# Experts on plain float32 matmuls, zero rows earlier, the last bias on VectorE

## The chip, the cores and the metric

The kernel runs on one core of a Trainium2 chip. The metric is the device time of one execution in microseconds. The kernel before took 3154.27 us in the median of three runs (3150.88 to 3159.85). One further execution was recorded with the hardware profiler; all rows come from it.

## The reference, cut to what matters

The input x has 16 sequences of 512 rows of 256 numbers (8192 rows). With a layer norm before each half, the reference computes

```
xn = layernorm(x)
x  = x + fast_weights(xn) + ffn(xn)
xn = layernorm(x)
x  = x + attention(xn, 16 heads) + ternary_ffn(xn)

def ffn(u):                                  # 16 routed experts, 2 chosen per row
    s = softmax(u @ centroids.T + expert_biases)
    g = the two largest s of a row, at their experts, 0 elsewhere
    routed = sum_e g[e] * (u @ Wr[e].T + br[e])
    return u + routed + mean over 2 shared experts of (u @ Ws.T + bs)

def ternary_ffn(z):
    w = +1 / 0 / -1 by a threshold of 0.7 * mean(|weight|)
    return z @ (w * alpha).T + bias
```

All of it is float32. The attention normalises its input to unit root mean square first (rms_norm).

## The kernel before, in words

The program has four blocks, one after the other, each of which ends when all engines and all its transfers are done.

*route* (the sorting stage, L115 to L710) goes over 32 units of two row tiles (256 rows). It normalises rows, scores experts, computes the fast-weight part and the shared experts, and sends each normalised row by indirect DMA to two places in `rows_dram`, where each expert has a region of its own. The end of an expert's rows has to be filled with zero rows up to a full tile of 128. SyncE runs the loads and stores in the order of the code: for each step `v` of a software pipeline the store of `part`, loads, and at step `NU` the two transfers of the job table; behind all steps it waits for the scatters and then stores 16 blocks of zero rows, one per expert, at places that it reads from `ends_u` into a register (L264 to L266). The expert weights are loaded to `raw` during this stage.

*experts* (L713 to L864) goes over 144 jobs in 72 pairs. A job is a tile of 128 rows of one expert. First ScalarE rounds the weights to the reduced type float32r (`wr_hi`, L792) and VectorE subtracts to get the rest (`wr_lo`, L814), 8 pieces each; then both do the same for the row of biases (L795, L816). Per pair, TensorE transposes two tiles (L840), ScalarE makes `xt_hi` and VectorE `xt_lo` of them (L800, L820), and per tile TensorE reads the expert's column into a register (`value_load`, L855) and issues seven float32r matmuls of 256 columns: the bias through a selecting matrix (L857), then for both halves of the 256 inputs hi x hi, hi x lo, lo x hi (L861 to L863). ScalarE copies even pairs out of PSUM (L806), VectorE odd ones (L826). SyncE loads tiles three pairs ahead into a ring of eight (L758, a register load before each) and stores each pair (L770); its order is: two loads, wait for the copied pair, store. PSUM holds three pairs of results, so TensorE's pair n waits for the copy of pair n - 3.

*settle* (L867 to L1081) goes over 32 units of two tiles. VectorE adds the parts and the two gathered results of each row, computes mean and variance (L1016 to L1034), then calls `finish` for the unit before: it makes `xrt_lo` (L1000), waits for TensorE's eight matmuls with the ternary weights (L1079, L1080), and writes `base` (L1007); then it computes six small factors of its own unit (L1038 to L1047), for which GpSimd supplies two powers (L973, L974). GpSimd also adds the last bias (L976) and issues four indirect gathers (L961). ScalarE applies the factors (L986) and copies the transposed rows (L992). SyncE stores them and loads three units ahead.

*phase_b* is the attention, unchanged.

Of the kernel before, what the change touches and what calls it, by code (L numbers as in the profile page):

```python
# [21 lines left out]
F32 = mybir.dt.float32  # L22
# [5 lines left out]
P = 128  # L28
D = 256
# [79 lines left out]
def route(nc, io, rows, part, region, jobs, kept, raw, raw_in):  # L109
# [5 lines left out]
    with ExitStack() as ctx:  # L115
# [105 lines left out]
        def _(sp):  # L221
# [23 lines left out]
            for v in steps:  # L245
# [10 lines left out]
                if v == NU:  # L256
                    sp.wait_ge(tb_dve, 13)
                    for k in range(2):
                        sp.dma_start(kept.table[0:1, k * 2 * P:(k + 1) * 2 * P].rearrange("a (p h) -> a p h", p=P),
                                     jobs_u[:, k]).then_inc(tb_in, 16)  # L260

            for r in range(XN):
                sp.wait_ge(sent[r], 16 * TOP * TB * len(range(r, GN, XN)))
            for e in range(NE):  # L264
                at = sp.value_load(ends_u[0:1, e:e + 1], min_val=0, max_val=NE * region - P)
                sp.dma_start(rows[bass.ds(at, P), :], zeros[:]).then_inc(ends_in, 16)  # L266
# [446 lines left out]
def experts(nc, io, rows, results, region, jobs, kept, raw, raw_in):  # L713
    with ExitStack() as ctx:
# [6 lines left out]
        def bank(name, n=1):  # L721
# [15 lines left out]
        place_pool, br_in, zero_pool, split_act, split_dve, t_pe, t_act, t_dve, y_pe, y_act, y_dve = map(sem, (  # L737
            "place_pool", "br_in", "zero_pool", "split_act", "split_dve", "t_pe", "t_act", "t_dve", "y_pe", "y_act", "y_dve"))
        PAIRS = jobs // U
        CUT = 4  # L740
        WIDE = NE * D // CUT

# [11 lines left out]
        def _(sp):  # L754
# [5 lines left out]
            sp.dma_start(raw_br[:], io["br"].rearrange("(a e) n -> a (e n)", a=1)).then_inc(br_in, 16)  # L760
            for j in range(3 * U):
                load(j)
            for n in range(PAIRS):
                for t in range(U):
                    load((n + 3) * U + t)
                if n % 2 == 0:
                    need(sp, y_act, 1, n // 2, 1)
                else:
                    need(sp, y_dve, 1, n // 2, 1)
# [5 lines left out]
        def _(g):  # L775
            g.memset(brow[:].bitcast(F32), 0.0).then_inc(zero_pool, 1)
# [9 lines left out]
        @block.scalar  # L786
        def _(a):
            a.wait_ge(raw_in, 16 * 16)
            for c in range(CUT):
                for k in range(KD):  # L790
                    cols = slice(c * WIDE, (c + 1) * WIDE)
                    a.activation(wr[0][:, k, cols], raw[:, k, cols], ACT.Copy).then_inc(split_act, 1)  # L792
            a.wait_ge(zero_pool, 1)
            a.wait_ge(br_in, 16)
            a.activation(brow[0:1, :], raw_br[:], ACT.Copy).then_inc(split_act, 1)  # L795
            for n in range(PAIRS + 1):
                if n < PAIRS:
# [69 lines left out]
def settle(nc, io, results, part, xT_hi, xT_lo, base_dram, early, kept):  # L867
    NU = part.shape[0]
    with ExitStack() as ctx:
# [37 lines left out]
        def flat(ap):  # L907
            return ap.rearrange("p a b c -> p (a b c)")
# [820 lines left out]
```

## Time and profile before

| | us |
|---|---|
| median of three timed runs | 3154.27 |
| the profiled execution | 3168.83 |
| its span | 3167.0 |
| sorting stage, from 0 to | 401.3 |
| experts' stage, to | 637.5 |
| settling stage, to about | 932 |
| attention, to | 3167.0 |

The profiled execution took 14.6 us longer than the median of the timed runs. TensorE is busy for 89% of the span, and its granted clock was 0.939 of full speed in the mean; of the two levels, 1.2 and 2.4 GHz, a clock of 0.5 in a stretch is the lower and 1.0 the upper. A stage's limit has to be read in the stage itself, since the shares of the whole span are those of the attention, which is 70% of it.

### The profile page before, as it was taken

How to read it: one execution, taken by the hardware profiler on the slowest of the kernel's cores; microseconds unless marked ns; L12 is line 12 of the kernel's file. 1: busy time of each engine (PE TensorE's matmuls, PEld its weight loads, DVE VectorE, ACT ScalarE, POOL GpSimd, SP SyncE). 2: the span in 40 equal slices, each digit the busy share in tenths (PEclk: the TensorE clock that was granted, in tenths of full speed). 3: DMA queues.
4: the chain of work that ended last, by engine and by line, in shares of the span. 5: the costliest groups of instructions: out<-in, count | busy, mean ns of one | idle time of the engine just before them, and what ended most of it. 6: DMA issues, size and time to landing. Idle time of an engine off the chain costs nothing.

```text
span 3167.0 us, 48881 instructions
## 1 busy us (share of the span) xinstructions
PE 2803.9 (89%) x14290; PEld 2132.5 (67%) x14290; DVE 2115.3 (67%) x3500; ACT 1864.8 (59%) x2685; POOL 2058.2 (65%) x1314
## 2 busy tenths in 40 slices
PE   5888668834448999999999999999999999999997
PEld 4777557723336677777777777777777777777775
DVE  6888443356766666766767667677676667667664
ACT  4555232211126777777767767777776777777674
POOL 4666330077744777777777777777777777777775
PEclk8999879955559999999999999999999999999999
DMA  3432245577751222223222222222222232232222
GB/s 120 134 122 85 87 131 181 172 219 214 211 176 44 61 50 72 60 57 77 45 72 61 60 73 50 68 54 71 54 64 73 44 77 55 62 77 47 70 56 46
DMA packets 266847, 281.05 MB, mean 89 GB/s; under 512 B 96755, under 2 KB 205555, under 8 KB 266740
## 3 DMA queue, kind: packets, MB, share of 16 engines
q1 hardware_dynamic: 254452, 246.17, 29.4%
q0 software_dynamic: 12288, 33.57, 3.4%
q8 instruction: 54, 0.88, 0.1%
q14 instruction: 53, 0.43, 0.0%
HBM read 129.67 MB, written 82.31 MB: 67 GB/s over the span
## 4 chain that ended last, share of the span: by engine, by line
PE 66%; ACT 1%; DVE 1%; DMA 1%; POOL 1%; issue 1%; SPq 0%; POOLq 0%; ACTq 0%; DVEq 0%
PE psV_b L1601 7%; PE psV_b L1596 7%; PE psV_b L1597 7%; PE psS_b L1584 7%; PE psS_b L1583 7%; PE psN_b L1569 7%; PE psY_b L1524 4%; PE psX_b L1524 4%; PE psY_b L1525 4%; PE psY_b L1526 4%; PE psX_b L1525 4%; PE psX_b L1526 4%; POOL pp_lo_b L1314 1%; DMA xT_lo<-xT_lo_dram 1%; PE psN_b L1653 0%
## 5 line engine op out<-in xcount | busy, mean ns | idle before, releaser
L1314 POOL TENSOR_TENSOR pp_lo_b<-pf_b,pp_hi_b 128x1024 fp32r<-128x1024 f32 x512 | 1229.8, 2402 | 609.0 <-ACT pp_hi_b L1356 522.9
L1460 DVE TENSOR_REDUCE negmax_b<-psN_b 128x2 fp32r<-128x1024 f32 x512 | 627.2, 1225 | 379.2 <-PE psN_b L1569 371.6
L1351 ACT ACTIVATE pf_b<-psS_b 128x1024 f32<-128x1024 f32 x512 | 526.1, 1028 | 239.0 <-PE psS_b L1584 235.9
L1583 PE MATMUL psS_b<-qA_b,kA_b 128*128 128x512 f32 x1024 | 405.8, 396 | 6.6 <-DVE qB_b L1475 4.7
L1584 PE MATMUL psS_b<-qB_b,kB_b 68*128 68x512 f32 x1024 | 406.5, 397 | 0.0
L1597 PE MATMUL psV_b<-pp_hi_b,vals_lo_b 128*64 128x512 f32 x1024 | 403.8, 394 | 0.0
L1596 PE MATMUL psV_b<-pp_hi_b,vals_hi_b 128*65 128x512 f32 x1024 | 402.0, 393 | 1.5
L1569 PE MATMUL psN_b<-kA_b,qA_b 128*128 128x512 f32 x1024 | 322.7, 396 | 4.7 <-DVE negmax_b L1460 4.6
L1601 PE MATMUL psV_b<-pp_lo_b,vals_hi_b 128*65 128x512 f32 x1024 | 320.2, 394 | 5.0 <-POOL pp_lo_b L1314 5.0
L1375 ACT ACTIVATE kA_b<-psX_b 64x512 fp32r<-64x512 f32 x256 | 152.1, 594 | 290.0 <-PE psX_b L1526 285.1
L1356 ACT ACTIVATE pp_hi_b<-pf_b 128x1024 fp32r<-128x1024 f32 x256 | 271.5, 1060 | 8.1
L1449 DVE SCALAR_TENSOR_TENSOR kB_b<-psX_b,kA_b 64x512 fp32r<-64x512 f32 x256 | 176.2, 688 | 140.5 <-ACT kA_b L1375 136.5
L1583 PEld LDWEIGHTS psS_b<-qA_b,kA_b 128*128 128x128 f32 x1024 | 193.6, 189 | 65.6 <-DVE qB_b L1475 7.0
L1470 DVE CAST pp_hi_b<-pf_b 128x1024 fp32r<-128x1024 f32 x256 | 232.9, 910 | 5.3 <-ACT pf_b L1351 5.3
L1569 PEld LDWEIGHTS psN_b<-kA_b,qA_b 128*128 128x128 f32 x1024 | 192.2, 190 | 55.2 <-DVE negmax_b L1460 7.8
L1524 PE MATMUL psX_b<-xT_hi,wqkv_hi_b 128*128 128x512 f32 x512 | 210.7, 412 | 15.1 <-DVE wqkv_lo_b L1435 9.6
L1328 POOL TENSOR_TENSOR otf_b<-outs,inverse_b 128x512 f32<-128x512 f32 x128 | 210.3, 1643 | 18.5 <-DMA inverse_b<-inverse_dram 15.1
L1584 PEld LDWEIGHTS psS_b<-qB_b,kB_b 68*128 68x128 f32 x1024 | 193.6, 189 | 40.5
L1601 PEld LDWEIGHTS psV_b<-pp_lo_b,vals_hi_b 128*65 128x65 f32 x1024 | 137.9, 135 | 105.3 <-POOL pp_lo_b L1314 8.9
L1525 PE MATMUL psX_b<-xT_lo,wqkv_hi_b 128*128 128x512 f32 x512 | 203.8, 398 | 0.0
L1526 PE MATMUL psX_b<-xT_hi,wqkv_lo_b 128*128 128x512 f32 x512 | 203.4, 397 | 0.0
L1475 DVE TENSOR_TENSOR qB_b<-psN_b,own_tile_b 4x512 fp32r<-4x512 f32 x256 | 173.3, 677 | 43.0 <-PE psN_b L1653 40.7
(243 smaller groups left out, 6123.1 us busy)
## 6 DMA issues: line engine op xcount, KB each, us to landing
kA_b<-kA_b SPq DMA_DIRECT2D x128, 256.0 KB, 3.2
qB_b<-qA_b SPq DMA_DIRECT2D x128, 256.0 KB, 2.9
inverse_b<-inverse_dram SPq DMA_DIRECT2D x256, 128.0 KB, 3.1
xs_e<-rows_dram SPq DMA_DIRECT2D x144, 128.0 KB, 2.1
results_dram<-ys_e SPq DMA_DIRECT2D x72, 256.0 KB, 2.3
x_a<-x_dram SPq DMA_DIRECT2D x16, 512.0 KB, 4.7
part_dram<-acc_a SPq DMA_DIRECT2D x32, 256.0 KB
acc_s<-part_dram SPq DMA_DIRECT2D x32, 256.0 KB
```

What stands on the lines that cost most here:

```text
L1314: pool.tensor_tensor(pp[1][:, c], pf[:, c], pp[0][:, c].bitcast(F32), ALU.subtract).then_inc(pl_pool, 1)
L1351: a.activation(pf[:, c], psS[:], ACT.Exp).then_inc(exp_act, 1)
L1460: v.tensor_reduce(negmax[:, n.slot(2), 2 * c:2 * c + 2], psN[:], AX.X, ALU.max, negate=True).then_inc(mx_dve, 1)
L1524: pe.matmul(out, lh, rh, start=start, stop=False)
L1525: pe.matmul(out, lh, rl, start=False, stop=False)
L1526: return pe.matmul(out, ll, rh, start=False, stop=stop)
L1569: mm = pe.matmul(psN[:, t], qA[:, s, i * P:(i + 1) * P], kA[:, s], start=True, stop=True)
L1583: pe.matmul(psS[:, t], kA[:, s, keys], qA[:, s], start=True, stop=False)
L1584: mm = pe.matmul(psS[:, t], kB[:, s, keys], qB[:, s], start=False, stop=True)
L1596: pe.matmul(psV[0:DH + 1, g.slot(2)], values(0, h, i), pp[0][:, c, t], start=(i == 0), stop=False)
L1597: pe.matmul(psV[0:DH, g.slot(2)], values(1, h, i), pp[0][:, c, t], start=False, stop=False)
L1601: mm = pe.matmul(psV[0:DH + 1, g.slot(2)], values(0, h, i), pp[1][:, c, t], start=False, stop=(i == TB - 1))
```

## The change

It has four parts. The 16 stores of zero rows go out in the last two steps of the sorting stage, eight each. In the experts' stage the weights are used as they were loaded: plain float32 matmuls, two per tile, without the conversion of weights and biases and without `xt_lo`; the biases of all experts are loaded to every partition (`bias_bc`), and VectorE adds them when it copies a result out of PSUM, one tile at a time, at a column that it reads into a register. In the settling stage GpSimd's two powers become one instruction of twice the columns, the add of the last bias goes from GpSimd to VectorE, and `finish` is cut in two: `xrt_lo` stays where it was, and `base` is written behind the factors.

```diff
+                if NU <= v < NU + 2:
+                    for e in range((v - NU) * NE // 2, (v - NU + 1) * NE // 2):
+                        at = sp.value_load(ends_u[0:1, e:e + 1], min_val=0, max_val=NE * region - P)
+                        sp.dma_start(rows[bass.ds(at, P), :], zeros[:]).then_inc(ends_in, 16)
 
             for r in range(XN):
                 sp.wait_ge(sent[r], 16 * TOP * TB * len(range(r, GN, XN)))
-            for e in range(NE):
-                at = sp.value_load(ends_u[0:1, e:e + 1], min_val=0, max_val=NE * region - P)
-                sp.dma_start(rows[bass.ds(at, P), :], zeros[:]).then_inc(ends_in, 16)
...
-        wr = [sb(f"wr_{p}", [P, KD, NE * D], F32R) for p in ("hi", "lo")]
-        brow = sb("brow", [P, NE * D], F32R)
-        raw_br = sb("raw_br", [1, NE * D])
+        bias_bc = sb("bias_bc", [P, NE * D])
         xs = sb("xs", [P, XS, D])
-        xt = [sb(f"xt_{p}", [P, 2, U, KD, P], F32R) for p in ("hi", "lo")]
+        xt = sb("xt", [P, 2, U, KD, P])
...
-            sp.dma_start(raw_br[:], io["br"].rearrange("(a e) n -> a (e n)", a=1)).then_inc(br_in, 16)
             for j in range(3 * U):
                 load(j)
+            sp.dma_start(bias_bc[:], io["br"].rearrange("e n -> (e n)").partition_broadcast(P)).then_inc(br_in, 16)
             for n in range(PAIRS):
                 for t in range(U):
                     load((n + 3) * U + t)
-                if n % 2 == 0:
-                    need(sp, y_act, 1, n // 2, 1)
-                else:
-                    need(sp, y_dve, 1, n // 2, 1)
+                need(sp, y_dve, U, n, U)
...
-            a.wait_ge(raw_in, 16 * 16)
-            for c in range(CUT):
-                for k in range(KD):
-                    cols = slice(c * WIDE, (c + 1) * WIDE)
-                    a.activation(wr[0][:, k, cols], raw[:, k, cols], ACT.Copy).then_inc(split_act, 1)
-            a.wait_ge(zero_pool, 1)
-            a.wait_ge(br_in, 16)
-            a.activation(brow[0:1, :], raw_br[:], ACT.Copy).then_inc(split_act, 1)
-            for n in range(PAIRS + 1):
-                if n < PAIRS:
-                    need(a, t_pe, 1, n, 1)
-                    need(a, y_pe, 1, n - 2, 1)
-                    a.activation(flat(xt[0][:, n % 2]), psT[:, n % 2], ACT.Copy).then_inc(t_act, 1)
-                m = n - 1
-                if m >= 0 and m % 2 == 0:
-                    need(a, y_pe, 1, m, 1)
-                    if m >= 4:
-                        a.wait_ge(y_out[m % 4], 16 * (m // 4))
-                    a.activation(ys[:, m % 4].rearrange("p a b -> p (a b)"), psY[:, m % 3], ACT.Copy).then_inc(y_act, 1)
+            for n in range(PAIRS):
+                need(a, t_pe, 1, n, 1)
+                need(a, y_pe, 1, n - 2, 1)
+                a.activation(flat(xt[:, n % 2]), psT[:, n % 2], ACT.Copy).then_inc(t_act, 1)
...
-            for c in range(CUT):
-                for k in range(KD):
-                    cols = slice(c * WIDE, (c + 1) * WIDE)
-                    v.wait_ge(split_act, c * KD + k + 1)
-                    v.tensor_tensor(wr[1][:, k, cols], raw[:, k, cols], wr[0][:, k, cols].bitcast(F32), ALU.subtract).then_inc(split_dve, 1)
-            v.wait_ge(split_act, CUT * KD + 1)
-            v.tensor_tensor(brow[32:33, :], raw_br[:], brow[0:1, :].bitcast(F32), ALU.subtract).then_inc(split_dve, 1)
             for n in range(PAIRS + 1):
-                if n < PAIRS:
-                    need(v, t_act, 1, n, 1)
-                    v.tensor_tensor(flat(xt[1][:, n % 2]), psT[:, n % 2], flat(xt[0][:, n % 2]).bitcast(F32), ALU.subtract).then_inc(t_dve, 1)
                 m = n - 1
-                if m >= 0 and m % 2 == 1:
+                if m >= 0:
+                    at = [v.value_load(kept.table[0:1, m * U + t:m * U + t + 1], min_val=0, max_val=(NE - 1) * D) for t in range(U)]
+                    if m == 0:
+                        v.wait_ge(br_in, 16)
                     need(v, y_pe, 1, m, 1)
                     if m >= 4:
                         v.wait_ge(y_out[m % 4], 16 * (m // 4))
-                    v.tensor_copy(ys[:, m % 4].rearrange("p a b -> p (a b)"), psY[:, m % 3]).then_inc(y_dve, 1)
+                    for t in range(U):
+                        v.tensor_tensor(ys[:, m % 4, t], psY[:, m % 3, t * D:(t + 1) * D], bias_bc[:, bass.ds(at[t], D)],
+                                        ALU.add).then_inc(y_dve, 1)
...
+                    need(pe, t_act, 1, n - 2, 1)
...
-            pe.wait_ge(split_dve, CUT * KD + 1)
+            pe.wait_ge(raw_in, 16 * 16)
             for n in range(PAIRS):
                 turn(n + 1)
-                need(pe, t_dve, 1, n, 1)
-                if n >= 3:
-                    if (n - 3) % 2 == 0:
-                        need(pe, y_act, 1, (n - 3) // 2, 1)
-                    else:
-                        need(pe, y_dve, 1, (n - 3) // 2, 1)
+                need(pe, t_act, 1, n, 1)
+                need(pe, y_dve, U, n - 3, U)
                 for t in range(U):
                     j = n * U + t
                     at = pe.value_load(kept.table[0:1, j:j + 1], min_val=0, max_val=(NE - 1) * D)
                     out = psY[:, n % 3, t * D:(t + 1) * D]
-                    pe.matmul(out, kept.pick[:], brow[:, bass.ds(at, D)], start=True, stop=False)
                     for k in range(KD):
-                        left = [part[:, n % 2, t, k] for part in xt]
-                        right = [part[:, k, bass.ds(at, D)] for part in wr]
-                        pe.matmul(out, left[0], right[0], start=False, stop=False)
-                        pe.matmul(out, left[0], right[1], start=False, stop=False)
-                        mm = pe.matmul(out, left[1], right[0], start=False, stop=(k == KD - 1))
+                        mm = pe.matmul(out, xt[:, n % 2, t, k], raw[:, k, bass.ds(at, D)], start=(k == 0), stop=(k == KD - 1))
...
-            g.wait_ge(const_in, 16)
             for u in range(NU):
                 need(g, s_dve, SD, u, 9)
                 need(g, s_dve, SD, u - 2, SD)
-                g.tensor_tensor(vs[:, u % 2, 0], mv[:, u % 2, :, 1], eps[:], ALU.add).then_inc(s_pool, 1)
+                g.tensor_tensor(vs[:, u % 2], mv[:, u % 2, :, 1].unsqueeze(1).to_broadcast([P, 2, U]), eps[:], ALU.add).then_inc(s_pool, 1)
                 need(g, s_pool, SP, u, 1)
-                g.tensor_tensor(root[:, u % 2, 0], vs[:, u % 2, 0], power[:, 0], ALU.pow).then_inc(s_pool, 1)
-                g.tensor_tensor(root[:, u % 2, 1], mv[:, u % 2, :, 1], power[:, 1], ALU.pow).then_inc(s_pool, 1)
-                need(g, o_dve, U, u - 3, U)
-                g.tensor_tensor(x1b[:, u % 3], x1[:, u % 3], fbias_bc[:].unsqueeze(1).to_broadcast([P, U, D]),
-                                ALU.add).then_inc(s_pool, 1)
+                g.tensor_tensor(flat2(root[:, u % 2]), flat2(vs[:, u % 2]), flat2(power[:]), ALU.pow).then_inc(s_pool, 1)
                 gather(u + 3)
...
+            def rows_low(u):
+                if u < 0:
+                    return
+                need(v, t_act, 1, u, 1)
+                if u >= 2:
+                    v.wait_ge(stored[u % 2], 80 * (u // 2))
+                v.tensor_tensor(flat(xrt[1][:, u % 2]), psT[:, u % 2], flat(xrt[0][:, u % 2]).bitcast(F32),
+                                ALU.subtract).then_inc(t_dve, 1)
+
             def finish(u):
                 if u < 0:
                     return
-                need(v, t_act, 1, u, 1)
-                v.tensor_tensor(flat(xrt[1][:, u % 2]), psT[:, u % 2], flat(xrt[0][:, u % 2]).bitcast(F32),
-                                ALU.subtract).then_inc(t_dve, 1)
-                need(v, s_pool, SP, u, 4)
-                if u >= 2:
-                    v.wait_ge(stored[u % 2], 80 * (u // 2))
                 need(v, f_pe, 1, u, 1)
                 for t in range(U):
                     v.scalar_tensor_tensor(out=base[:, u % 2, t], in0=psF[:, u % 2, t * D:(t + 1) * D], scalar=fac[:, u % 3, 5, t:t + 1],
                                            in1=x1b[:, u % 3, t], op0=ALU.mult, op1=ALU.add).then_inc(o_dve, 1)
 
+            v.wait_ge(const_in, 16)
...
+                need(v, s_pool, SP, u - 2, 2)
                 for t in range(U):
                     v.bn_aggr(mv[:, u % 2, t], stats[:, u % 2, t]).then_inc(s_dve, 1)
-                finish(u - 1)
+                rows_low(u - 1)
+                v.tensor_tensor(x1b[:, u % 3], x1[:, u % 3], fbias_bc[:].unsqueeze(1).to_broadcast([P, U, D]),
+                                ALU.add).then_inc(s_dve, 1)
                 f = fac[:, u % 3]
-                need(v, s_pool, SP, u, 3)
+                need(v, s_pool, SP, u, 2)
                 v.tensor_tensor(f[:, 0], root[:, u % 2, 0], root[:, u % 2, 1], ALU.mult).then_inc(s_dve, 1)
...
                 v.scalar_tensor_tensor(out=f[:, 4], in0=mv[:, u % 2, :, 0], scalar=-1.0, in1=f[:, 3],
                                        op0=ALU.mult, op1=ALU.mult).then_inc(s_dve, 1)
+                finish(u - 1)
+            rows_low(NU - 1)
             finish(NU - 1)
```

## Rows read from the trace of the kernel before

**Rows 1.** Windows by stage: start:end, length; busy (instructions) per engine; clock, DMA share, GB/s.

```profile
401.30:425.00 23.70, 8.53 (x39) 7.77 (x40) 16.11 (x12) 13.46 (x13) 22.21 (x18) 0.51 0.20 58
425.00:630.00 205.00, 182.07 (x1237) 152.31 (x1236) 71.38 (x104) 58.54 (x103) 8.94 (x16) 0.99 0.57 175
...
650.00:925.00 275.00, 122.83 (x496) 98.69 (x496) 190.14 (x573) 53.73 (x96) 206.00 (x247) 0.54 0.68 205
```

**Rows 2.** SyncE's two DMA lines: count, ns min/median/max, first to last start.

```profile
L758 SPq DMA_DIRECT2D xs_e<-rows_dram x144: 332/333/1283, 402.9 to 625.9; - x144
...
L770 SPq DMA_DIRECT2D results_dram<-ys_e x72: 360/383/1208, 422.7 to 634.9; - x72
```

**Rows 3.** Timeline of TensorE, experts (start us, us, instruction): full clock, then half clock.

```profile
501.89 0.60 PE L840 MATMUL psT_e<-ident_f,xs_e 128*128 128x128 f32 x4
...
504.43 0.28 PE L862 MATMUL psY_e<-wr_lo_e,xt_hi_e 128*128 x1
504.55 0.28 PE L863 MATMUL psY_e<-wr_hi_e,xt_lo_e 128*128 x1
504.67 0.60 PE L840 MATMUL psT_e<-ident_f,xs_e 128*128 128x128 f32 x4
...
446.71 0.41 PE L863 MATMUL psY_e<-wr_hi_e,xt_lo_e 128*128 x1
446.92 0.41 PE L857 MATMUL psY_e<-brow_e,pick 128*128 x1
```

**Rows 4.** Timeline of SyncE's queue, end of sorting and first experts.

```profile
376.96 1.22 SPq L259 DMA_DIRECT2D table<-jobs_u_a  x2
...
382.79 16.71 SPq L266 DMA_DIRECT2D rows_dram<-zeros_a  x16
...
402.93 8.04 SPq L758 DMA_DIRECT2D xs_e<-rows_dram  x8
...
426.07 0.38 SPq L770 DMA_DIRECT2D results_dram<-ys_e  x1
427.20 1.43 SPq L758 DMA_DIRECT2D xs_e<-rows_dram  x2
428.68 0.43 SPq L770 DMA_DIRECT2D results_dram<-ys_e  x1
```

**Rows 5.** VectorE's first add of a settling unit: count, ns, first to last start.

```profile
L1016 DVE TENSOR_TENSOR acc_s<-psA_s,x_s x32: 691/692/693, 649.6 to 914.1; 128x512 f32<-128x512 f32 x32
```

**Rows 6.** Timeline of one unit of the settling stage.

```profile
768.31 0.69 DVE L1016 TENSOR_TENSOR acc_s<-psA_s,x_s 128x512 f32<-128x512 f32 x1
...
771.88 0.66 DVE L1000 TENSOR_TENSOR xrt_lo_s<-psT_s,xrt_hi_s 128x512 fp32r<-128x512 f32 x1
...
772.32 0.73 POOL L973 TENSOR_TENSOR root_s<-vs_s,power_s 128x2 f32<-128x2 f32 x1
...
774.25 0.41 PE L1080 MATMUL psF_s<-wtern,xrt_lo_s 128*128 128x256 f32 x1
...
774.81 0.88 DVE L1007 SCALAR_TENSOR_TENSOR base_s<-psF_s,fac_s,x1b_s 128x256 f32<-128x256 f32 x2 [2.27 <-DMA xT_lo_dram<-xrt_lo_s]
...
775.60 0.15 DVE L1038 TENSOR_TENSOR fac_s<-root_s 128x2 f32<-128x2 f32 x1
...
776.91 0.69 DVE L1016 TENSOR_TENSOR acc_s<-psA_s,x_s 128x512 f32<-128x512 f32 x1
```

**Rows 7.** DMA throughput of the first 40 us, in 40 slices of 1 us.

```profile
GB/s 0 8 63 370 386 364 229 63 135 235 348 361 366 374 368 344 337 319 312 253 122 378 60 0 0 0 0 0 0 48 241 236 0 0 8 0 0 0 0 0
```

**Rows 8.** Groups of TensorE, sorting stage, 80 to 340: count, busy us, mean ns.

```profile
L706 PE MATMUL psB_a<-th_a,w_a 128*128 128x256 f32 x206 | 52.9, 379 | 0.0
...
L704 PE MATMUL psB_a<-pick,bshare_a 128*128 128x256 f32 x52 | 14.7, 283 | 0.0
```

**Rows 9.** Two lines of GpSimd: count, ns min/median/max, first to last start.

```profile
L334 POOL TENSOR_TENSOR rstd_a<-rstd_a,power_a x16: 1007/1008/1040, 7.3 to 302.3; 128x4 f32<-128x4 f32 x16
...
L782 POOL TENSOR_TENSOR moved_e<-moved_e,shift_e x15: 453/458/4663, 408.9 to 434.5; 128x128 f32<-128x128 f32 x15
```

More of the change, by code:

```diff
@@ L736, in experts @@
         y_out = [sem(f"y_out{i}") for i in range(4)]
-        place_pool, br_in, zero_pool, split_act, split_dve, t_pe, t_act, t_dve, y_pe, y_act, y_dve = map(sem, (
-            "place_pool", "br_in", "zero_pool", "split_act", "split_dve", "t_pe", "t_act", "t_dve", "y_pe", "y_act", "y_dve"))
+        place_pool, br_in, t_pe, t_act, y_pe, y_dve = map(sem, (
+            "place_pool", "br_in", "t_pe", "t_act", "y_pe", "y_dve"))
         PAIRS = jobs // U
-        CUT = 4
-        WIDE = NE * D // CUT
         def flat(ap):
@@ L775, in _ @@
         def _(g):
-            g.memset(brow[:].bitcast(F32), 0.0).then_inc(zero_pool, 1)
             g.tensor_copy(moved[:], kept.place_f[:]).then_inc(place_pool, 1)
@@ L834, in turn @@
                         need(pe, x_in[j % XS], 16, j // XS, 16)
-                    need(pe, t_dve, 1, n - 2, 1)
+                    need(pe, t_act, 1, n - 2, 1)
                     for t in range(U):
@@ L881, in settle @@
         power = sb("power", [P, 2, U])
-        eps = sb("eps", [P, U])
+        eps = sb("eps", [P, 2, U])
         acc = sb("acc", [P, 4, U, D])
@@ L903, in settle, with flat2 @@
             "const_in", "const_pool", "s_dve", "s_pool", "p_pe", "x_act", "t_pe", "t_act", "t_dve", "f_pe", "o_dve"))
-        SD = 5 + 2 + 2 + 6
-        SP = 4
+        SD = 5 + 2 + 2 + 1 + 6
+        SP = 2
         def flat(ap):
             return ap.rearrange("p a b c -> p (a b c)")
+        def flat2(ap):
+            return ap.rearrange("p a b -> p (a b)")
         block = ctx.enter_context(nc.Block())
@@ L950, in _ @@
         def _(g):
-            for tile, value in ((power[:, 0], -0.5), (power[:, 1], 0.5), (eps[:], 1e-5)):
+            for tile, value in ((power[:, 0], -0.5), (power[:, 1], 0.5), (eps[:, 0], 1e-5), (eps[:, 1], 0.0)):
                 g.memset(tile, value).then_inc(const_pool, 1)
-            g.wait_ge(const_pool, 3)
+            g.wait_ge(const_pool, 4)
             def gather(u):
@@ L1013, in _ @@
                 need(v, x_act, U, u - 3, U)
-                need(v, s_pool, SP, u - 3, 4)
                 need(v, p_pe, 1, u, 1)
@@ L1031, in _ @@
                 need(v, s_dve, SD, u, 7)
-                need(v, s_pool, SP, u - 2, 3)
+                need(v, s_pool, SP, u - 2, 2)
                 for t in range(U):
                     v.bn_aggr(mv[:, u % 2, t], stats[:, u % 2, t]).then_inc(s_dve, 1)
-                finish(u - 1)
+                rows_low(u - 1)
+                v.tensor_tensor(x1b[:, u % 3], x1[:, u % 3], fbias_bc[:].unsqueeze(1).to_broadcast([P, U, D]),
+                                ALU.add).then_inc(s_dve, 1)
                 f = fac[:, u % 3]
-                need(v, s_pool, SP, u, 3)
+                need(v, s_pool, SP, u, 2)
                 v.tensor_tensor(f[:, 0], root[:, u % 2, 0], root[:, u % 2, 1], ALU.mult).then_inc(s_dve, 1)
-                need(v, s_dve, SD, u, 10)
+                need(v, s_dve, SD, u, 11)
                 v.tensor_scalar(f[:, 1], f[:, 0], 1e-12 * float(D) ** -0.5, None, ALU.max).then_inc(s_dve, 1)
-                need(v, s_dve, SD, u, 11)
+                need(v, s_dve, SD, u, 12)
                 v.reciprocal(f[:, 2], f[:, 1]).then_inc(s_dve, 1)
                 v.tensor_scalar(f[:, 5], f[:, 1], kept.alpha_bc[:, 0:1], None, ALU.mult).then_inc(s_dve, 1)
-                need(v, s_dve, SD, u, 13)
+                need(v, s_dve, SD, u, 14)
                 v.tensor_tensor(f[:, 3], f[:, 2], root[:, u % 2, 0], ALU.mult).then_inc(s_dve, 1)
-                need(v, s_dve, SD, u, 14)
+                need(v, s_dve, SD, u, 15)
                 v.scalar_tensor_tensor(out=f[:, 4], in0=mv[:, u % 2, :, 0], scalar=-1.0, in1=f[:, 3],
                                        op0=ALU.mult, op1=ALU.mult).then_inc(s_dve, 1)
+                finish(u - 1)
+            rows_low(NU - 1)
             finish(NU - 1)
```

## The prediction, written before the result was known

> **What bounds the kernel now.** I read the page first: its forty slices show four stretches, a sorting stage to about 401 us, the experts' stage to about 637, a settling stage to about 932, and attention behind it, where TensorE is busy nine tenths and more. The edit touches the first three, so I asked for the windows of these stages. The reader is to see that TensorE is busy 182 of 205 us among the experts at full clock (0.99), and only 123 of 275 us in the settling stage, at half clock (0.54), where VectorE (190) and GpSimd (206) do more [rows 1]. Attention has 70% of the span and no instruction of it changes, so its time is carried over.
>
> Then I read each stage in order of time. *Experts:* 72 pairs of row tiles. The results of a pair are stored once per pair; first and last of these stores give (634.9 - 422.7) / 71 = 2.99 us per pair [rows 2]. A smooth pair is 504.67 - 501.89 = 2.78 us on TensorE [rows 3]: four transposes, 4 x (0.60 - 0.28) / 3 = 0.43 until the next may start, then per tile seven records at a pitch of 0.118 (0.83). The rest, 2.78 - 0.43 - 1.65 = 0.70, is idle around the two register loads that fetch the expert's column. SyncE runs nearly as long: store to store is 2.61 us where it never waits (426.07 to 428.68: 1.13 to the first load, 1.43 for two loads, 0.05) [rows 4]. *Settling:* 32 units in a loop that VectorE closes; 31 intervals take 914.1 - 649.6 = 264.5 us, 8.53 each, and the typical one 776.91 - 768.31 = 8.60 [rows 5, 6]. In it VectorE waits 2.27 us before L1007. The profile names a DMA of an older unit, but the last matmul into psF ends at 774.25 + 0.41 = 774.66, 0.15 before VectorE goes on, so it is the matmuls it waits for [rows 6].
>
> **Part 1, zero rows.** Before, SyncE issues the sixteen stores in (16.71 - 0.33) / 15 = 1.09 us each from 382.79, and the stage ends at 401.3, 1.8 us behind the last issue [rows 4, 1]. Now eight follow the table's transfers (done at 376.96 + 1.22 = 378.18), the last part store goes between (0.6), then the other eight: 378.2 + 16 x 1.09 + 0.6 + 1.8 = 398.1. Nothing on SyncE is behind them but the waits for scatters already sent, and the part store, 6 us later than before, is read only in the settling stage. **Saves 3.2 us**; bounds 0 (the stores held back by something else) and 4.6 (382.79 - 378.18).
>
> **Part 2, start of the experts.** Before, the first store goes 422.7 - 401.3 = 21.4 us into the stage: eight conversions on ScalarE and eight on VectorE, then the bias row, then 3.5 us of matmuls at half clock [rows 2, 1]. All that goes. What is late next is a new transfer: the biases on every partition, 128 x 16 KB = 2.1 MB, queued behind six loads. The loads start at 1.6 - 0.3 = 1.3 us, go out every (8.04 - 0.33) / 7 = 1.10 [rows 4], the last at 6.8; the bias is issued at about 7.3. The fastest slices at the kernel's start move 340 to 386 GB/s [rows 7]; at 366 the bias takes 5.7 us, with 2 us of landing (2.1 median for a load [rows 2]) it is there at 15. Pair 0's matmuls are done by about 12 even at half clock, so the bias ends last: two adds and the first store at 15.9. Loads 6 and 7 land behind the bias, at about 15, when TensorE wants them. **Saves 5.5 us**; bounds 0 (the bias at the 175 GB/s of this stage [rows 1] takes 12 us: store at 22) and 9 (only pair 0 decides).
>
> **Part 3, a pair in the steady stage.** Removed per tile: the bias matmul and six f32r records of 0.118. Added: two plain float32 matmuls. The sorting stage has this shape (L706, 128x128 by 128x256): 206 records stand there beside 52 of L704, where the code issues two plain ones for each, so a plain matmul is two records [rows 8]. Four records take 1.03 us and one 0.379, so the pitch is (1.03 - 0.379) / 3 = 0.217, and one plain matmul 0.434, against 3 x 0.118 = 0.354 for the three it replaces [rows 8, 3]. Per pair: 8 x 0.217 = 1.74 against 14 x 0.118 = 1.65. So the arithmetic gets 0.09 dearer, not cheaper; the gain must come from the idle 0.70. In the half-clock stretch at 446 us, records have a pitch of 0.21, and the second tile's L857 starts 0.21 behind the L863 before it, with no idle at all: the register load is done while slow records are still queued [rows 3]. Plain records are as slow (0.217) at full clock. I take 0.1 of the 0.70 as left: 0.43 + 1.74 + 0.1 = 2.27 us; bounds 2.2 and, nothing hidden, 2.87.
>
> VectorE gets all evictions: two adds of 128x256 from PSUM, which I put at 0.75 together (a 128x512 add from PSUM takes 0.69 at L1016 [rows 5]; bounds 0.69 and 0.88, the two of L1007 [rows 6]), and two register loads that lie before its wait for TensorE; with L820 gone it has room in 2.6 us. ScalarE keeps one copy. Then SyncE is late next: 2.61 us without a wait, more with its own slow issues (a load's issue is 0.333 median but 1.283 at most, a store's 0.383 and 1.208 [rows 2]); I add 0.14 for these. So 2.75 a pair: 71 x (2.99 - 2.75) = **17 us saved**. Bounds: 27 (2.61), and -6 (TensorE 2.87 and the 0.21 by which mean and smooth pair differ today: 3.08).
>
> **Part 4, settling.** VectorE's unit before: from the add at 768.31 to L1000's end at 772.54 are 4.23 us, then 2.27 of wait, 0.8 to the first small factor operation at 775.60, and 1.31 for the six of them [rows 6]. After: L1000, then the add of the bias (SBUF only, 128x512; 0.69 as L1016 [rows 5], bounds 0.6 and 0.88, the two of L1007 for as many columns [rows 6]), then the six factors, then the wait for psF, then L1007. GpSimd: its two powers (0.73 and 0.69) become one of four columns, which takes 1.008 in the sorting stage (L334 [rows 9]); it starts as today 4.01 into the unit (772.32) and ends at 5.0. Factors: 5.1 + 1.31 = 6.4. The matmuls start as today and end at 774.66 - 768.31 = 6.35, so L1007 may start at 6.5 as today. It takes 0.88, then the next unit: 7.4; with some friction 7.45. Its four transposes run on TensorE behind the matmuls, at the half-clock pitch of 0.21 [rows 3] some 0.9 us, to 7.25. GpSimd, busy 206 / 275 x 8.53 = 6.4 us of a unit [rows 1], loses the bias add and part of a power from that. The DMA engines go from 0.68 busy [rows 1] to 0.68 x 8.53 / 7.45 = 0.78. 31 intervals: 264.5 - 31 x 7.45 = 33.5, and the last unit gains some 1.5, as its factors no longer stand behind L1007. **Saves 35 us**; bounds 15 (below) and 41 (7.3 a unit).
>
> **Sum.** 3.2 + 5.5 + 17 + 35 = 61 us. The profiled execution took 3168.8 us (span 3167.0), so one like it would take 3108. It lies 14.6 above the median of the three timed runs; I take 61 from that median: 3154.3 - 61 = **3093 us**.
>
> **Rivals.**
> *A, TensorE stays the bound among the experts.* For it: plain matmuls are dearer, and the idle at the register loads may be latency that no queue hides. Against it: the gapless stretch [rows 3]. The 17 go: 3110, and 3116 at the lower bound.
> *B, the add moved to VectorE blocks GpSimd.* While VectorE ran L814 and L816 (two inputs from SBUF), GpSimd's L782, 0.458 in the median, took 4.66 [rows 9]. If the new add stops the power for its 0.65 us, the factors start at 5.8, end at 7.1, and L1007 closes the unit at 8.05: part 4 saves 264.5 - 31 x 8.05 = 15, and the time is 3113. Against it: a power computes long on few elements, and L334 ran beside VectorE's small SBUF adds in 1.007 to 1.040 each time [rows 9]. Beside this, the Trainium skill (GPSIMD Engine Reference, Specifications) says that GpSimd's SBUF interface is shared with VectorE and contended by VectorE's instructions "with two SBUF inputs"; by that rule the unit would be this rival's 8.05, and L782's row agrees that the rule is real here.
> *C, slower: the experts run at half clock.* The clock falls for 3 us in that stage behind a pause of TensorE (446 us: pitch 0.21 [rows 3]). The new stage starts at half clock and pauses for the bias. If it stays there, a pair costs 8 x 0.434 + 4 x 0.22 + 0.1 = 4.45 us: 71 x (4.45 - 2.99) = +104, less 3.2, 5.5 and 35, gives 3214. It decides from 3.8 us a pair on. Against it: at half clock TensorE has no idle left, and today, with matmuls from about 4 us before the first store, the windows show full clock from 425 on [rows 1].
> *D, nothing ends earlier*, the freed time going into waits for DMA: 3154.
>
> **Chances.** Forecast 0.58, A 0.14, B 0.16, A and B together 0.05 (3130), C 0.04, D 0.03. For 8 in 10 the range holds the forecast's own bounds and most of A and B: 3070 (parts at their better bounds: 4.6 + 9 + 27 + 41 = 82 less) to 3128. A measurement here tells 0.3%, about 9.5 us, from no change; faster 0.93, within 0.3% 0.03, slower 0.04.
>
> **What would show it.** Zero stores that end near 396 and experts' first load before 400. First store to results 16 us into the stage; if 22, the bias. Store to store 2.6 to 2.8 with TensorE idle before its transposes, waiting for xs (SyncE binds); idle before the first matmul of a tile instead is A. A unit of 7.4 to 7.5 us in the settling stage with almost no wait before the adds that L1007 makes today; the power at 1.0 us, or 1.6 for B. Granted clock of the experts under 0.8 is C. A changed attention stage would make all of it wrong.

## The result, and the profile after

The changed kernel took 3103.45 us (median of four runs, 3094.51 to 3110.58) against 3156.93 for the kernel before (four, 3150.88 to 3159.85). The ratio is 0.9832, with a 95% interval of 0.9801 to 0.9862. The prediction was 3093 (3070 to 3128) and faster; from median to median the change saved 53.5 us where 61 were forecast. The profiled execution took 3110.6 us (span 3108.8) where it said 3108 for one like that of before. The total hides two errors against each other, so the stages have to be read one by one. All comparisons from here are between profiled executions.

The windows answer to [rows 1]: start:end, length, then busy us (instructions) of PE, PEld, DVE, ACT and POOL, then clock, DMA share, GB/s.

```profile
391.90:407.20 15.30, 8.84 (x29) 6.74 (x30) 0.75 (x2) 1.79 (x3) 13.06 (x23) 0.58 0.59 207
...
415.60:613.70 198.10, 171.37 (x812) 122.35 (x812) 51.52 (x137) 40.01 (x67) 0.00 (x0) 1.00 0.57 179
628.10:853.70 225.60, 117.66 (x481) 95.24 (x482) 199.25 (x587) 51.76 (x92) 154.54 (x182) 0.61 0.81 246
```

The experts ran at full clock from 415.6 on (1.00), and the settling stage's DMA share rose to 0.81 (0.68 before). Next, SyncE's stores [rows 2] and VectorE's first add of a unit [rows 5], two answers of the line view:

```profile
L764 SPq DMA_DIRECT2D results_dram<-ys_e x72: 360/433/1795, 407.2 to 613.7; - x72
...
L981 DVE TENSOR_TENSOR acc_s<-psA_s,x_s x32: 681/692/693, 628.1 to 853.7; 128x512 f32<-128x512 f32 x32
```

A pair takes (613.7 - 407.2) / 71 = 2.91 us, before 2.99, and a settling unit (853.7 - 628.1) / 31 = 7.28, before 8.53. SyncE's queue from the end of sorting to the first pairs [rows 4]:

```profile
370.23 1.23 SPq L259 DMA_DIRECT2D table<-jobs_u_a  x2
...
382.06 7.95 SPq L264 DMA_DIRECT2D rows_dram<-zeros_a  x8
393.12 5.87 SPq L755 DMA_DIRECT2D xs_e<-rows_dram  x6
399.04 0.43 SPq L759 DMA_DIRECT2D bias_bc_e<-br_dram  x1
...
407.24 0.39 SPq L764 DMA_DIRECT2D results_dram<-ys_e  x1
```

The table went out 6.7 us earlier than in the profile of before (370.23 against 376.96). Nothing ahead of it was changed, and x1_three_act_store below, which has the sorting stage of before, sends it at 368.36; all nine profiles but that of before lie between 367.8 and 372.4. So that is variation between executions, and I measure part 1 from the table. The whole account of the two spans, with predictions:

| | before | after | saved | predicted |
|---|---|---|---|---|
| sorting up to the table's transfer | 377.0 | 370.2 | 6.7 | 0 |
| table to start of the experts' stage | 24.3 | 21.7 | 2.7 | 3.2 |
| stage start to first store | 21.4 | 15.3 | 6.1 | 5.5 |
| first to last store | 212.2 | 206.5 | 5.7 | 17 |
| last store to first settling add | 14.7 | 14.4 | 0.3 | 0 |
| 31 settling intervals, then to the last base add | 264.5 + 14.6 | 225.6 + 12.3 | 41.2 | 35 |
| last base add to the end | 2238.3 | 2242.8 | -4.5 | 0 |

The sum is 58.2, the difference of the spans (3167.0 - 3108.8). The four parts gave 55.7 where 61 were forecast; part 3 fell short by 11 and part 4 gave 6 more.

### The profile page after: what moved, and what is told of

Read it like the earlier page. It is cut to its first block, busy times and chain, and to the rows that moved or that the text cites. A ratio compares the mean times of both kernels' runs of the same rounds, so it can differ in the third digit from the quotient of the medians.

```text
span 3108.8 us, 48109 instructions
## 1 busy us (share of the span) xinstructions
PE 2798.6 (90%) x13858; PEld 2106.4 (68%) x13858; DVE 2095.9 (67%) x3559; ACT 1834.0 (59%) x2640; POOL 1999.1 (64%) x1250
## 4 chain that ended last, share of the span: by engine, by line
PE 67%; DMA 1%; ACT 1%; DVE 1%; POOL 1%; issue 1%; SPq 0%; POOLq 0%; ACTq 0%; DVEq 0%
PE psV_b L1570 7%; PE psV_b L1565 7%; PE psV_b L1566 7%; PE psS_b L1553 7%; PE psS_b L1552 7%; PE psN_b L1538 7%; PE psY_b L1493 4%; PE psX_b L1493 4%; PE psY_b L1494 4%; PE psY_b L1495 4%; PE psX_b L1494 4%; PE psX_b L1495 4%; DMA xT_lo<-xT_lo_dram 1%; POOL pp_lo_b L1283 1%; PE psN_b L1622 0%
## 5 line engine op out<-in xcount | busy, mean ns | idle before, releaser
L1297 POOL TENSOR_TENSOR otf_b<-outs,inverse_b 128x512 f32<-128x512 f32 x128 | 217.0, 1695 | 11.6 <-DMA inverse_b<-inverse_dram 10.0
L1493 PE MATMUL psX_b<-xT_hi,wqkv_hi_b 128*128 128x512 f32 x512 | 210.9, 412 | 14.5 <-DVE wqkv_lo_b L1404 9.0
```

What stands on the lines that cost most here:

```text
L1493: pe.matmul(out, lh, rh, start=start, stop=False)
```

## Part 3: what a pair waits for

The timeline of the changed kernel shows three consecutive pairs (start us, us, instruction). It answers to [rows 3].

```profile
480.63 0.44 SPq L764 DMA_DIRECT2D results_dram<-ys_e  x1
481.82 1.46 SPq L755 DMA_DIRECT2D xs_e<-rows_dram  x2
...
483.32 0.43 SPq L764 DMA_DIRECT2D results_dram<-ys_e  x1
484.87 1.44 SPq L755 DMA_DIRECT2D xs_e<-rows_dram  x2
485.09 0.42 PEld L813 LDWEIGHTS psT_e<-ident_f,xs_e 128*128 128x128 f32 x4 [0.20 <-issue]
486.00 0.73 PEld L827 LDWEIGHTS psY_e<-wr_raw,xt_e 128*128 128x128 f32 x4 [0.49 <-issue]
486.35 0.43 SPq L764 DMA_DIRECT2D results_dram<-ys_e  x1
486.89 0.73 PEld L827 LDWEIGHTS psY_e<-wr_raw,xt_e 128*128 128x128 f32 x4 [0.16 <-issue]
487.53 1.43 SPq L755 DMA_DIRECT2D xs_e<-rows_dram  x2
488.16 0.76 DVE L798 TENSOR_TENSOR ys_e<-psY_e,bias_bc_e 128x256 f32<-128x256 f32 x2 [1.97 <-PE psY_e L827]
489.00 0.43 SPq L764 DMA_DIRECT2D results_dram<-ys_e  x1
```

Follow one chain. Store at 480.63; the loads behind it in SyncE's order from 481.82, out by 483.28; landed about 485.0, 2.0 behind the issue of the second (the median of the landings); transposes at 485.09; matmuls 486.00 to 488.0; adds 488.16 to 488.92; store 489.00. That is 8.37 us, and the store at its end is the third after the one at its start: loads run three pairs ahead, and TensorE's program puts the transposes of pair n + 3 before the matmuls of pair n + 2. So a chain closes on itself over three pairs, at 8.37 / 3 = 2.79 here.

But SyncE's queue closes at the same height. In these three pairs it never waits for a result: 484.87 + 1.44 = 486.31 and the store at 486.35, 487.53 + 1.43 = 488.96 and the store at 489.00. Two of the three rounds take 2.69 and 2.65, and the one of 3.03 has a longer stretch in front of its first load (1.12 after the store's issue, in the other two 0.75). TensorE meanwhile waits before its transposes (0.20; "issue" is here a transfer that has not landed). The two tiles of a pair follow each other without a gap in its matmuls (486.00 + 0.73 + 0.16 = 486.89), so the register load is hidden there; only the one behind the short transposes still shows (0.49).

Where SyncE does wait for a result, a slow issue or register load has gone before in most cases, as here, where two loads took 2.50 us instead of 1.43 and the next but one store waits 1.36:

```profile
413.74 2.50 SPq L755 DMA_DIRECT2D xs_e<-rows_dram  x2
416.28 0.43 SPq L764 DMA_DIRECT2D results_dram<-ys_e  x1
417.46 1.43 SPq L755 DMA_DIRECT2D xs_e<-rows_dram  x2
420.25 0.38 SPq L764 DMA_DIRECT2D results_dram<-ys_e  x1
...
605.95 8.09 SPq L764 DMA_DIRECT2D results_dram<-ys_e  x4
```

Of the 71 intervals the first 68 contain two loads, the last three none: (605.95 - 407.24) / 68 = 2.92 us. In 46 of these 68 pairs the store follows its loads at once (0.04 to 0.07), in 22 it waits, 0.13 us a pair in the mean over all. So 2.92 is 2.79 of SyncE's own time and 0.13 of waits. In the kernel before the same reading gives 2.75 and 0.25.

The theory for the experiments, called L in them, is the latency loop alone. Rival T is TensorE as the bound at 2.9, and rival S slow issues of SyncE.

**e1_deep.** A ring of 16 row tiles, loads six pairs ahead:

```
-        XS = 8
+        XS = 16
...
+            for j in range(3 * U, 6 * U):
+                load(j)
             for n in range(PAIRS):
                 for t in range(U):
-                    load((n + 3) * U + t)
+                    load((n + 6) * U + t)
```

> The changed kernel with a ring of 16 input tiles and loads six pairs ahead of the store, not three; nothing else. The changed kernel takes 2.91 us from store to store among the experts, where 2.75 was predicted. Theory L (a closed loop of latencies: store of pair n-1, two loads, landing, transposes, matmuls, eviction, store of pair n+2, some 8.7 us over three pairs): twice the lead halves what the loop asks, so the next limit shows, SyncE's own queue: 2.65 to 2.75 a pair, 11 to 18 us off the stage. Theory T (TensorE with register loads that are not hidden, 2.9 of its own): 2.9, nothing gained. Theory S (SyncE's queue is simply busy for 2.9): 2.9, nothing gained.

It took 3089.87 us in one run. Its stores:

```profile
L766 SPq DMA_DIRECT2D results_dram<-ys_e x72: 359/434/1472, 407.0 to 597.5; - x72
```

```profile
587.72 1.43 SPq L755 DMA_DIRECT2D xs_e<-rows_dram  x2
589.19 8.62 SPq L766 DMA_DIRECT2D results_dram<-ys_e  x7
```

(597.5 - 407.0) / 71 = 2.68 us, which seems to be within what L said. But the last seven stores go out with no load between them. The 65 intervals before them take (589.19 - 407.0) / 65 = 2.80 us, and in none of them does a store follow its loads by more than 0.07. So 2.80 is the pace of SyncE's queue, 2.67 in the median of the store intervals and slow issues on top. Of the 16 us that the stage gained, 8 are in these 65 pairs (2.92 before) and 8 in the last six intervals, 8.3 us instead of 16.7, where results lay ready. L is confirmed only in part: the loop adds about 0.12 a pair. T is out (see e2), and S is nearer than L: SyncE is busy for 2.80 of the 2.92.

**e3_lead2.** The other direction: `load((n + 2) * U + t)`, and four loads ahead instead of six.

> The changed kernel with loads two pairs ahead of the store, not three. Theory L: the same 8.7 us now go over two pairs, 4.3 us a pair, the stage about 100 us longer. Theories T and S: the work of TensorE and of SyncE is unchanged, so 2.9 a pair and the time of the changed kernel.

It took 3218.51 us:

```profile
L764 SPq DMA_DIRECT2D results_dram<-ys_e x72: 360/383/865, 407.2 to 727.3; - x72
```

(727.3 - 407.2) / 71 = 4.51 us, 9.0 for two pairs, near the 8.7 (3 x 2.91) that three pairs take in the changed kernel. No busy engine would show that: with two pairs of lead the loop alone binds, while with three it is about as long as three rounds of SyncE.

**e2_act_store.** The stores go to ScalarE's queue, two pairs behind its copies; SyncE only loads.

```
+            for n in range(PAIRS + 2):
+                if n < PAIRS:
...
+                if n >= 2:
+                    need(a, y_dve, U, n - 2, U)
+                    a.dma_start(out_dram[n - 2], ys[:, (n - 2) % 4]).then_inc(y_out[(n - 2) % 4], 16)
```

> The changed kernel with the stores of results issued by ScalarE, so that SyncE only loads (ring of eight, as before) and no load stands behind a store. Theory L: neither the loop nor SyncE's queue (2.2 us for two loads) binds; what is left is TensorE, 0.43 of transposes, 1.74 of matmuls and what is then left idle at the register loads, 0.1 to 0.5: 2.3 to 2.65 a pair, 18 to 40 us off the stage. Theory T: 2.9 stays. Theory S: 2.3, as TensorE's queue would hide the register loads.

It took 3066.59 us, 37 less than the changed kernel's median. The stores, and TensorE in one smooth stretch:

```profile
L783 ACTq DMA_DIRECT2D results_dram<-ys_e x72: 366/367/642, 406.0 to 573.6; - x72
```

```profile
470.52 0.60 PE L814 MATMUL psT_e<-ident_f,xs_e 128*128 128x128 f32 x4
470.96 1.89 PE L828 MATMUL psY_e<-wr_raw,xt_e 128*128 x8
472.69 0.60 PE L814 MATMUL psT_e<-ident_f,xs_e 128*128 128x128 f32 x4
```

A pair is (573.6 - 406.0) / 71 = 2.36 us in the mean and 472.69 - 470.52 = 2.17 in the smooth stretch: 0.43 + 8 x 0.217, with no idle left. T is out; L and S both allowed 2.3, so this run doesn't tell them apart. TensorE's best pair is 0.10 below the prediction's 2.27, and in it both register loads are hidden. Over 425 to 570 the waits in front of the first matmuls still add up to 14.5 us, 0.24 a pair.

**x1_three_act_store.** The same edit on the kernel before, with its three f32r matmuls and the bias matmul. It asks whether the shape of the matmuls brings anything.

> The kernel before (three f32r matmuls and a bias matmul per tile) with one edit: the experts' result stores are issued by ScalarE, so that SyncE issues loads alone and the loop stores - loads - transposes is open, as in the run of the changed kernel that took 2.36 us a pair with stores on ScalarE. Theory H (with the loop open, the shape of the matmuls decides: short records don't cover TensorE's register loads, 0.70 us of idle a pair stay): 2.75 to 2.85 us a pair, TensorE idle 0.3 before each tile's first matmul, total 3157 - 72 x 0.15 to 0.22 = 3141 to 3147. Rival N (plain matmuls bring nothing, only the loop matters): 2.35 to 2.5 a pair and about 3115 to 3125.

It took 3157.41 us, no gain. Its stores, and TensorE's largest wait from 425 to 610 (us in total, times, longest):

```profile
L795 ACTq DMA_DIRECT2D results_dram<-ys_e x72: 366/366/1682, 414.0 to 621.3; - x72
```

```profile
PEld psY_e L863 <- issue: 46.0, 127, 1.0
```

2.92 us a pair, above even H's 2.85, and the total lies above H's 3141 to 3147; N's 2.35 to 2.5 is far off. In the 185 us of the window (some 63 pairs) 46.0 are idle before the first matmul of a tile, 0.73 a pair: the 0.70 of the prediction. TensorE waits for nothing else there; 0.43 + 1.65 + 0.73 = 2.81 leaves 0.11 unexplained. So opening SyncE's order does nothing for this idle, and plain matmuls do: 0.24 a pair in e2. The two experiments together say where the expected gain went: the edit moved TensorE's limit from about 2.8 to 2.17 in its best pair, but only 0.08 of it could be had before the next limits, SyncE's queue and the loop.

## Parts 1 and 2: the start of the experts

In the changed kernel the first adds end VectorE's wait for the bias, 7.4 us behind its issue at 399.04:

```profile
406.45 0.76 DVE L798 TENSOR_TENSOR ys_e<-psY_e,bias_bc_e 128x256 f32<-128x256 f32 x2 [36.25 <-DMA bias_bc_e<-br_dram]
```

**e4_bias_early.** The broadcast moves into sorting steps 16 to 23, in eight pieces:

```
+                if 16 <= v < 24:
+                    cols = slice((v - 16) * NE * D // 8, (v - 15) * NE * D // 8)
+                    sp.dma_start(bias_bc[:, cols], io["br"].rearrange("e n -> (e n)")[cols].partition_broadcast(P)).then_inc(br_in, 16)
```

> The changed kernel with the broadcast of the biases taken out of the experts' stage: it is loaded in eight pieces during the sorting stage. Theory (the bias landing, 7.4 us behind its issue, sets the first store at 15.3 us into the stage): without it the first store goes out 11 to 13 us into the stage, and the total falls by 2.5 to 4 us. Rival (loads 6 and 7 or the half clock of TensorE set it): first store at 15 as now and no gain. The steady pair stays at 2.9 by both.

It took 3091.74 us in one run. Its first adds and first stores:

```profile
402.36 0.76 DVE L799 TENSOR_TENSOR ys_e<-psY_e,bias_bc 128x256 f32<-128x256 f32 x2 [32.46 <-PE psY_e L828]
```

```profile
392.80 8.07 SPq L757 DMA_DIRECT2D xs_e<-rows_dram  x8
403.14 0.39 SPq L765 DMA_DIRECT2D results_dram<-ys_e  x1
```

TensorE now ends the wait, the first store goes out some 11 us into the stage, and from the first load to the first store it is 10.3 us instead of 14.1 (407.24 - 393.12): 3.8 saved, so the bias was indeed last in the changed kernel. The total fell by 11.7, not by 2.5 to 4. Between the profiled executions 8.8 us of it lie behind the last base add, where nothing differs, and 5.6 in the steady pairs (2.83 us instead of 2.91), which both theories had put at 2.9. Why these are shorter is open; one run can't tell it from variation.

**b1_two_queues.** All that the runs point to: the edits of e2 and e4, and half of the zero stores on ScalarE.

```
-                if NU <= v < NU + 2:
-                    for e in range((v - NU) * NE // 2, (v - NU + 1) * NE // 2):
+                if v == NU:
+                    for e in range(NE // 2):
...
+            for e in range(NE // 2, NE):
+                at = a.value_load(ends_u[0:1, e:e + 1], min_val=0, max_val=NE * region - P)
+                a.dma_start(rows[bass.ds(at, P), :], zeros[:]).then_inc(ends_in, 16)
```

> The version that the runs point to: the changed kernel with the experts' stores issued by ScalarE, the biases loaded during sorting, and eight of the sixteen zero stores issued by ScalarE beside SyncE's eight. Expected by terms: 3103 - 37 (stores on ScalarE, measured 3067) - 3 (bias early) - 5 to 9 (eight zero stores of 1.0 us each off SyncE's end of sorting) = 3054 to 3059. If the zero stores on two queues hide nothing: 3062 to 3064. Steady pair 2.36 us, settling unit 7.26. If the bias only shifts the wait to the first loads: first store 12 us into the stage or later.

It took 3057.33 us (3052.58 to 3061.61, four runs) beside 3156.98 for the kernel before: ratio 0.9681, 95% interval 0.9665 to 0.9698. It beats the changed kernel as well. SyncE's queue at the end of sorting, and the two groups:

```profile
367.90 1.22 SPq L262 DMA_DIRECT2D table<-jobs_u_a  x2
...
383.15 0.37 SPq L761 DMA_DIRECT2D xs_e<-rows_dram  x1
```

```profile
L788 ACTq DMA_DIRECT2D results_dram<-ys_e x72: 366/366/418, 393.7 to 562.7; - x72
...
L987 DVE TENSOR_TENSOR acc_s<-psA_s,x_s x32: 678/691/693, 578.1 to 803.2; 128x512 f32<-128x512 f32 x32
```

From the table to the first load it is 15.3 us where the changed kernel has 22.9: 7.6 less for eight stores of about 1.0 us taken off SyncE. Part 1 of the change had only moved the stores; they were still the path. Pairs take 2.38, units 7.26.

## Part 4: the settling unit

One unit of the changed kernel, its main instructions. It answers to [rows 6].

```profile
671.08 0.69 DVE L981 TENSOR_TENSOR acc_s<-psA_s,x_s 128x512 f32<-128x512 f32 x1
...
675.09 1.03 POOL L939 TENSOR_TENSOR root_s<-vs_s,power_s 128x4 f32<-128x4 f32 x1
675.22 0.68 DVE L1001 TENSOR_TENSOR x1b_s<-x_s,fbias_bc_s 128x512 f32<-128x512 f32 x1
...
676.16 0.16 DVE L1005 TENSOR_TENSOR fac_s<-root_s 128x2 f32<-128x2 f32 x1 [0.26 <-POOL root_s L939]
...
677.02 0.41 PE L1049 MATMUL psF_s<-wtern,xrt_lo_s 128*128 128x256 f32 x1
677.08 0.16 DVE L1014 SCALAR_TENSOR_TENSOR fac_s<-mv_s,fac_s 128x2 f32<-128x2 f32 x1
...
677.47 0.88 DVE L972 SCALAR_TENSOR_TENSOR base_s<-psF_s,fac_s,x1b_s 128x256 f32<-128x256 f32 x2 [0.24 <-PE psF_s L1049]
...
678.42 0.69 DVE L981 TENSOR_TENSOR acc_s<-psA_s,x_s 128x512 f32<-128x512 f32 x1
```

678.42 - 671.08 = 7.34 us, the usual length (median 7.33; the mean of 7.28 has some shorter units in it). The bias add (0.68) and the six factors (676.16 to 677.24) fill most of the time until psF is written at 677.43; 0.24 of the wait is left, and L972 follows at once: the prediction's picture. psF was ready 6.35 us into the unit, as said, and L972 started at 6.39 instead of 6.5. The factors took 1.08 (1.31 said), which changes nothing, since psF comes after them. The power runs beside the bias add and takes 1.03 us. Two runs undo one half of part 4 each.

**s1_order_only.** The new order stays; GpSimd keeps the bias add and its two powers.

```
...
-                g.tensor_tensor(flat2(root[:, u % 2]), flat2(vs[:, u % 2]), flat2(power[:]), ALU.pow).then_inc(s_pool, 1)
+                g.tensor_tensor(root[:, u % 2, 0], vs[:, u % 2, 0], power[:, 0], ALU.pow).then_inc(s_pool, 1)
+                g.tensor_tensor(root[:, u % 2, 1], mv[:, u % 2, :, 1], power[:, 1], ALU.pow).then_inc(s_pool, 1)
+                need(g, o_dve, U, u - 3, U)
+                g.tensor_tensor(x1b[:, u % 3], x1[:, u % 3], fbias_bc[:].unsqueeze(1).to_broadcast([P, U, D]),
+                                ALU.add).then_inc(s_pool, 1)
```

> The changed kernel, but in the settling stage GpSimd keeps the add of the last bias and the two powers; only the order on VectorE is new (base is written behind the factors). The whole change brought the unit from 8.53 to 7.28 us. If the order carries the gain: VectorE works 4.2 us, then has no bias add, and waits for the second power (ends 5.4 into the unit), factors to 6.7 at most, base from there: 7.2 to 7.6 a unit unless GpSimd binds, whose loop is 0.2 + 1.4 + 1.3 + 5.1 = 8.0 and would be the new limit: 8.0 to 8.1. If instead the moved add carries the gain, the unit stays at 8.5.

It took 3138.35 us. Three answers of the line view: the first add of a unit, VectorE's first factor, GpSimd's bias add.

```profile
L988 DVE TENSOR_TENSOR acc_s<-psA_s,x_s x32: 677/680/692, 628.4 to 883.7; 128x512 f32<-128x512 f32 x32
...
L1010 DVE TENSOR_TENSOR fac_s<-root_s x32: 1218/1235/1240, 633.9 to 889.0; 128x2 f32<-128x2 f32 x32
...
L943 POOL TENSOR_TENSOR x1b_s<-x_s,fbias_bc_s x32: 1250/1268/1272, 633.8 to 888.9; 128x512 f32<-128x512 f32 x32
```

A unit takes (883.7 - 628.4) / 31 = 8.24, so order alone brings 0.29 of the 1.25 us. The expectation put GpSimd's loop at 8.0 to 8.1; what else it cost is in the last section.

**s2_move_only.** The other half: `finish(u - 1)` stands behind `rows_low(u - 1)` again, ahead of the bias add and the factors, and GpSimd keeps its relief.

> The changed kernel with one thing undone: in a settling unit the two base adds (and their wait for psF) stand before the six factor operations again, as in the kernel before. The bias add stays on VectorE and GpSimd has one merged power. Theory O (each of the two halves of part 4 is needed; order alone gave 8.24 us a unit): VectorE's unit is its own 4.2 us to the end of xrt_lo, then psF is ready 6.5 us into the unit whatever stands before it (the bias add only fills 0.7 of the 2.3 us of wait), then 0.88 for the base adds and 1.0 to 1.2 for the factors, so 8.4 to 8.6 us a unit, as before (8.53), and the total is 3138 to 3150 (3103 + 31 x 1.1 to 1.3 + some for the tail). Rival G (relieving GpSimd is what carries part 4): 7.3 to 7.6 us a unit, total about 3105.

It took 3149.25 us:

```profile
L981 DVE TENSOR_TENSOR acc_s<-psA_s,x_s x32: 691/692/692, 627.5 to 898.4; 128x512 f32<-128x512 f32 x32
```

```profile
763.70 0.88 DVE L972 SCALAR_TENSOR_TENSOR base_s<-psF_s,fac_s,x1b_s 128x256 f32<-128x256 f32 x2 [2.17 <-PE psF_s L1049]
764.49 0.68 DVE L1002 TENSOR_TENSOR x1b_s<-x_s,fbias_bc_s 128x512 f32<-128x512 f32 x1
```

8.74 us a unit, 0.2 more than before the change. Against the expectation's words, the bias add doesn't fill the wait here: the edit puts it behind L972, so VectorE waits its full 2.17 us for psF and then pays 0.68 more. G's 7.3 to 7.6 is out: relief of GpSimd brings nothing with this order on VectorE. Moving one half brings 0.29 us, moving the other -0.21, and both 1.25. A third cut was not run: the old order with the bias add in front of the wait for psF. It would hide the 0.68, so I estimate 8.74 - 0.68 = 8.06 for it; most of the gain would still be missing.

## Why the prediction was right, and where it was not

- *Parts 1 and 2* held within 0.6 us each: the zero stores left the end of the stage by 2.7 (3.2 said), and the bias was late next, with the first store at 15.3 us (15.9 said). e4 shows the latter by taking the bias away.
- *Part 3* named the right engine and sized it too low: "Then SyncE is late next: 2.61 us without a wait ... So 2.75 a pair". SyncE's own time was 2.79 in the changed kernel and 2.80 in e1, and on top came 0.13 of waits for results, which the prediction put at nothing. They come from the chain store, loads, landing, transposes, matmuls, adds, store, which closes over three pairs. I had compared the busy time of queues and not followed a store to the store that waits for it. All its links were in the rows of before: 1.13 + 1.10 to the issue of the second load [rows 4] + 2.1 of landing + 0.43 and one register load's 0.35 + 1.74 [rows 3, 8] + about 0.9 for adds and their hand-over = 7.8, or 2.6 a pair with no friction: as much as SyncE's own 2.61. Two limits at one height need an allowance on top of either.
- *Rival A* (TensorE stays the bound) fits the number, 6 us instead of 17, by another cause, and the total came within the range partly by luck: part 3 fell 11 short and part 4 gave 6 more. e2 refutes A: with the same program on TensorE a pair takes 2.36. x1 shows the idle at the register loads staying with f32r matmuls.
- *Part 4* was right in mechanism. The usual unit came to 7.34 (7.45 said), because L972 followed psF by 0.04 instead of 0.15 and no friction was added. s1 and s2 show that neither half does it alone. The upper bound of 41 us didn't follow from its 7.3 a unit: 264.5 - 31 x 7.3 + 1.5 = 39.7.
- *Rival B* is refuted as it stood: the power takes 1.036 us in the median of 32 (1.467 at most) beside VectorE's two-input add, and 1.008 in the sorting stage [rows 9].
- *Rival C* didn't come: full clock from 415.6 on. *D* is out.
- Variation between executions (6.7 us before the table, -4.5 in attention) is of the size of parts 1 to 3 and cancels only in the median.

## What to carry over

Where loads and stores share one in-order queue, follow one store through everything that must happen until the next store that depends on it, and divide by the number of pairs of lead: that is a limit beside those of the engines, and it can be tested by changing the lead. When you read such a test, leave out the intervals at the end that have no loads in them: e1 gives 2.68 with them and 2.80 without. An instruction dear in itself (two plain float32 records of 0.217 against three of 0.118) can still be the faster one if it covers the register work between instructions. In a loop that one engine closes, filling its wait and shortening its supplier may pay far more together than apart, so cost each alone before you cost both.

## What was not expected of the hardware

In s1 VectorE's L1010, a product of two operands of 128x2, took 1.235 us in the median and at least 1.218 in all 32 cases, where the same operation (L1005) takes 0.161 in the changed kernel. It starts just behind GpSimd's bias add (L943, 1.268 us, both inputs in SBUF). In one unit:

```profile
765.42 1.27 POOL L943 TENSOR_TENSOR x1b_s<-x_s,fbias_bc_s 128x512 f32<-128x512 f32 x1
765.48 1.24 DVE L1010 TENSOR_TENSOR fac_s<-root_s 128x2 f32<-128x2 f32 x1 [1.22 <-POOL root_s L941]
```

Both end at 766.7. So the contention of rival B is there, in the other direction: GpSimd's add, which started first, holds VectorE's small product until it is done. The Trainium skill (SBUF — State Buffer, section "SBUF: two separate sides") says that the pair of ports that the two engines share goes to whichever starts first, for its whole instruction, where VectorE's has two inputs in SBUF and GpSimd's reads SBUF. The row agrees with it. By that sentence the power of the changed kernel would do the same to VectorE's bias add, which starts 0.13 us behind it (675.22 behind 675.09) with both inputs in SBUF; it doesn't. The add runs 0.68 us and is done before the power is. So here a power on 128x4 held nothing back, and an add on 128x512 did.

Moving the bias add to VectorE took this hold away as well as GpSimd's time; how the 0.96 us between s1 and the changed kernel split between the two was not measured. The hold delays the factors by 1.235 - 0.161 = 1.07 us. GpSimd's instructions in that unit of s1 wait 0.33 us for VectorE's mean and variance and 0.17 for its first factor, so without the hold GpSimd would still need about 8.24 - 0.50 = 7.7 us a unit. By this estimate the hold and GpSimd's own time have about half of the 0.96 each.
